# Moving the second horizontal product of a deformable convolution from VectorE to ScalarE, with the vertical mix one tap earlier

## What is computed

```
out_normal = conv(x, w_normal)
offset     = concat(conv(x, w_offx), conv(x, w_offy))       # 18 numbers a pixel
out_x      = deform_conv(x, offset, w_dx)
out_y      = deform_conv(x, offset, w_dy)
out        = relu(bn(conv(concat(out_normal, out_x, out_y), w_fusion)))
out        = relu(bn(conv(out, w_conv2)) + x)
# deform_conv: for each of 9 taps and each pixel, a bilinear sample
s = corner(y0, x0)*(1-ty)*(1-tx) + corner(y0, x0+1)*(1-ty)*tx
  + corner(y0+1, x0)*ty*(1-tx)   + corner(y0+1, x0+1)*ty*tx
out = einsum('bckhw,ock->bohw', s, w)
```

## Time and profile before

| what | value |
|---|---|
| median of 3 runs | 2600.68 us (2598.38 to 2600.81) |
| profiled execution, its own time | 2602.97 us |
| its span | 2601.2 us |
| busy in the span: PE, DVE, ACT, POOL | 91%, 87%, 60%, 74% |
| TensorE's granted clock, mean of the span | 0.961 |
| chain that ended last, by engine | DVE 46%, PE 23%, ACT 15%, issue 8%, DMA 5%, POOL 2% |

### The profile page before, as it was taken

One profiled execution on the slowest core, in us unless ns is written; L12 is line 12 of the kernel. 1 busy time (PEld: TensorE's weight loads), 2 busy tenths in 40 slices (PEclk: granted clock), 3 DMA queues, 4 the chain that ended last, 5 costly groups with the idle time before them and its releaser, 6 DMA issues.

```text
span 2601.2 us, 47091 instructions
## 1 busy us (share of the span) xinstructions
PE 2355.7 (91%) x15680; PEld 2319.4 (89%) x15680; DVE 2265.0 (87%) x5999; ACT 1561.9 (60%) x3577; POOL 1917.4 (74%) x1807
## 2 busy tenths in 40 slices
PE   3668999999999999999999999999999998999997
PEld 3668889898999999998999999999999998999997
DVE  5788988888999999999999989999999998999962
ACT  5777888778555555555555555555555555555531
POOL 7777777777777777777777777777777777777730
PEclk7789999999999999999999999999999999999998
DMA  7767777777777777777777777777777667776630
GB/s 232 220 208 219 235 228 231 232 231 229 227 237 233 231 234 237 233 236 232 236 237 237 234 237 239 238 222 210 209 209 217 206 208 212 210 210 210 202 111 26
DMA packets 179139, 564.90 MB, mean 217 GB/s; under 512 B 32720, under 2 KB 34128, under 8 KB 178768
## 3 DMA queue, kind: packets, MB, share of 16 engines
q0 software_dynamic: 144000, 471.97, 60.3%
q1 hardware_dynamic: 34896, 89.91, 10.1%
HBM read 527.41 MB, written 34.34 MB: 216 GB/s over the span
## 4 chain that ended last, share of the span: by engine, by line
DVE 46%; PE 23%; ACT 15%; issue 8%; DMA 5%; POOL 2%; ACTq 0%; DVEq 0%; SPq 0%; POOLq 0%
DVE mixed L756 11%; DVE d_lo L708 7%; DVE d_lo_f L832 7%; DVE samp L762 6%; ACT samp L535 6%; PE work L388 5%; PE work L394 5%; PE work L391 5%; DMA cells<-slope_table,index 4%; DVE samp_lo L708 4%; ACT samp_hi L534 3%; ACT mixed L535 3%; PE turned L431 2%; POOL cells L350 2%; PE acc L388 2%
## 5 line engine op out<-in xcount | busy, mean ns | idle before, releaser
L350 POOL DMA_INDIRECT cells<-slope_table,index x1350 | 1434.0, 1062 | 414.1 <-issue 223.3
L535 ACT ACTIVATE samp<-mixed,wgt 128x128 f32<-128x128 f32 x1800 | 644.6, 397 | 492.6 <-DVE mixed L756 490.8
L350 POOL DMA_INDIRECT cells<-in_xpair,index x450 | 473.7, 1053 | 166.6 <-issue 83.4
L756 DVE SCALAR_TENSOR_TENSOR mixed<-cells,wgt 128x256 f32<-128x256 f32 x1350 | 560.9, 477 | 39.2 <-DMA cells<-slope_table,index 37.9
L762 DVE SCALAR_TENSOR_TENSOR samp<-mixed,wgt,samp 128x128 f32<-128x128 f32 x1800 | 513.8, 345 | 39.1 <-ACT samp L535 38.8
L388 PE MATMUL work<-d_hi,w_hi 128*128 128x320 f32 x1440 | 467.9, 325 | 22.0 <-ACT off_s L534 19.7
L391 PE MATMUL work<-d_lo,w_hi 128*128 128x320 f32 x1440 | 452.8, 314 | 0.0
L394 PE MATMUL work<-d_hi,w_lo 128*128 128x320 f32 x1440 | 452.3, 314 | 0.0
L388 PE MATMUL acc<-samp_hi,w_hi 128*128 128x320 f32 x1440 | 450.2, 313 | 0.0
L391 PE MATMUL acc<-samp_lo,w_hi 128*128 128x320 f32 x1440 | 448.4, 311 | 0.0
L394 PE MATMUL acc<-samp_hi,w_lo 128*128 128x320 f32 x1440 | 446.9, 310 | 0.0
(11 more groups left out here) (86 smaller groups left out, 4279.3 us busy)
## 6 DMA issues: line engine op xcount, KB each, us to landing
cells<-slope_table,index POOLq DMA_INDIRECT x1350, 3.9
slope<-in_xpair SPq DMA_DIRECT2D x54, 384.0 KB, 5.3
slope_table<-slope SPq DMA_DIRECT2D x54, 384.0 KB, 4.1
x_raw<-in_xflat SPq DMA_DIRECT2D x40, 410.0 KB, 4.1
resid<-in_x SPq DMA_DIRECT2D x40, 320.0 KB, 5.3
out<-resid SPq DMA_DIRECT2D x40, 320.0 KB, 3.9
cells<-in_xpair,index POOLq DMA_INDIRECT x450, 3.8
w_lo_f<-in_weights SPq DMA_DIRECT2D x4, 576.0 KB, 7.9
```

The lines of the kernel that those rows point to most:

```text
L350: eng.indirect_dma_start(out=cells[:, g, :], out_offset=None, in_=cell_rows, in_offset=bass.IndirectOffsetOnAxis(ap=index[:, par, j, k:k + ...
L535: return eng.activation(dst, src, ACT.Copy, scale=scale)
L756: eng.scalar_tensor_tensor(out=both, in0=corner[:, g, :, 1, :], scalar=wgt[:, par, 1, 0, j, k:k + 1], in1=base, op0=ALU.mult, op1=ALU.add, ...
```

## The change

In images 1 to 3 (`n >= PLAIN`) ScalarE makes both horizontal products, in place in `mixed` (10 copies of 128 elements a tap), and VectorE adds them in a single instruction of 640 elements into `samp`. In image 0 the split stays as it was. `sample` is cut into `mix` and `blend`, and `mix` runs one tap earlier for all images: in step n VectorE does `blend(n + 2)`, `samples_low(n + 1)`, the indices if due, `mix(n + 3)`, and then its jobs. ScalarE does `samples_high(n + 1)`, then `across(n + 3)` and `upper(n + 4)`, and then its jobs. GpSimd, SyncE and TensorE keep their order; only the count that TensorE waits for differs (`samp_count`).

```diff
-                at_least(eng, samp_done, TILES * n + TILES)
+                at_least(eng, samp_done, samp_count(n + 1))
...
-            def left(n, k, par, tp):
-
-                at_least(eng, samp_turned, n - 1)
+            def across(n):
...
+                if n < PLAIN:
+                    at_least(eng, samp_turned, n - 1)
                 for j in range(TILES):
                     at_least(eng, mixed_done, TILES * n + j + 1)
-                    copy(samp[:, tp, j], mixed[:, tp, j, 0:C], scale=wgt[:, par, 0, 1, j, k:k + 1]).then_inc(left_done, 1)
+                    left, right = mixed[:, tp, j, 0:C], mixed[:, tp, j, C:2 * C]
+                    if n < PLAIN:
+                        copy(samp[:, tp, j], left, scale=wgt[:, c % 2, 0, 1, j, k:k + 1]).then_inc(left_done, 1)
+                    else:
+                        copy(left, left, scale=wgt[:, c % 2, 0, 1, j, k:k + 1]).then_inc(left_done, 1)
+                        copy(right, right, scale=wgt[:, c % 2, 1, 1, j, k:k + 1]).then_inc(left_done, 1)
...
                     n = i * TAPS + k
                     tp = (par + k) % 2
-                    if fl.strip and k < TAPS - 2:
-                        left(n + 2, k + 2, par, tp)
...
                     if fl.strip and (k < TAPS - 1 or fl.nxt):
                         samples_high(n + 1, 1 - tp)
...
-                        upper(n + 3, i, k + 3, par, 1 - tp)
...
+                    across(n + 3)
+                    upper(n + 4)
...
+            def blend(n):
...
+                if n >= PLAIN:
+                    at_least(eng, samp_turned, n - 1)
+                    at_least(eng, left_done, left_count(n + 1))
+                    combine(samp[:, tp], mixed[:, tp, :, 0:C], mixed[:, tp, :, C:2 * C], ALU.add).then_inc(samp_done, 1)
+                    return
...
-                        sample(n + 2, k + 2, par, tp)
...
+                    blend(n + 2)
                     if fl.strip and (k < TAPS - 1 or fl.nxt):
                         samples_low(n + 1, 1 - tp)
...
                     if k == fl.turn and fl.nxt:
                         indices(i + 1, 1 - par)
+                    mix(n + 3)
```

More of the change, by code:

```diff
@@ L63, with left_count, samp_count @@
 STEPS = NS + 4
+TOTAL = NS * TAPS
+PLAIN = STRIPS * TAPS
+def left_count(n):
+    return TILES * min(n, PLAIN) + 2 * TILES * max(n - PLAIN, 0)
+def samp_count(n):
+    return TILES * min(n, PLAIN) + max(n - PLAIN, 0)
 SLICES = [
@@ L557, in turned_evac, with upper @@
                     .then_inc(p_out, 1)
-            def upper(n, c, k, par, tp):
-                if c >= STRIPS:
+            def upper(n):
+                if n >= PLAIN:
                     return
-                at_least(eng, samp_done, TILES * (n - 1))
+                c, k, tp = n // TAPS, n % TAPS, n % 2
+                at_least(eng, samp_done, samp_count(n - 1))
                 for j in range(TILES):
@@ L567, in upper @@
                     copy(mixed[:, tp, j].rearrange("p (x c) -> p x c", x=2), corner[:, g, :, 0, :],
-                         scale=wgt[:, par, 0, 0, j, k:k + 1]).then_inc(upper_done, 1)
-            def left(n, k, par, tp):
-                at_least(eng, samp_turned, n - 1)
+                         scale=wgt[:, c % 2, 0, 0, j, k:k + 1]).then_inc(upper_done, 1)
+            def across(n):
+                if n >= TOTAL:
+                    return
+                c, k, tp = n // TAPS, n % TAPS, n % 2
+                if n < PLAIN:
+                    at_least(eng, samp_turned, n - 1)
                 for j in range(TILES):
                     at_least(eng, mixed_done, TILES * n + j + 1)
-                    copy(samp[:, tp, j], mixed[:, tp, j, 0:C], scale=wgt[:, par, 0, 1, j, k:k + 1]).then_inc(left_done, 1)
+                    left, right = mixed[:, tp, j, 0:C], mixed[:, tp, j, C:2 * C]
[4 more added lines that the diff above has]
+                        copy(right, right, scale=wgt[:, c % 2, 1, 1, j, k:k + 1]).then_inc(left_done, 1)
             def samples_high(n, tp):
@@ L597, in _ @@
             weights_high(W_DEF)
-            upper(0, 0, 0, 0, 0)
-            left(0, 0, 0, 0)
+            upper(0)
+            across(0)
             x_high(1, 1)
-            upper(1, 0, 1, 0, 1)
+            upper(1)
+            across(1)
+            upper(2)
             samples_high(0, 0)
-            left(1, 1, 0, 1)
-            upper(2, 0, 2, 0, 0)
+            across(2)
+            upper(3)
             eng.wait_ge(bn_step, 1)
@@ L625, in step @@
                     tp = (par + k) % 2
-                    if fl.strip and k < TAPS - 2:
-                        left(n + 2, k + 2, par, tp)
-                    elif fl.strip and fl.nxt:
-                        left(n + 2, k + 2 - TAPS, 1 - par, tp)
                     if fl.strip and (k < TAPS - 1 or fl.nxt):
@@ L633, in step @@
                         weights_high(fl.weights[k])
-                    if fl.strip and k < TAPS - 3:
-                        upper(n + 3, i, k + 3, par, 1 - tp)
-                    elif fl.strip and fl.nxt:
-                        upper(n + 3, i + 1, k + 3 - TAPS, 1 - par, 1 - tp)
                     if k == fl.turn and fl.nxt:
                         turned_evac(i + 1)
+                    across(n + 3)
+                    upper(n + 4)
                     if k == 1 and fl.last_row:
@@ L743, in indices, with combine, mix @@
                 eng.wait_ge(idx_ready, s + 1)
-            def sample(n, k, par, tp):
+            def combine(dst, a, b, op):
+                return eng.scalar_tensor_tensor(out=dst, in0=a, scalar=1.0, in1=b, op0=ALU.mult, op1=op)
+            def mix(n):
+                if n >= TOTAL:
+                    return
+                c, k, tp = n // TAPS, n % TAPS, n % 2
                 for j in range(TILES):
@@ L750, in sample @@
                     base = both
-                    if n < STRIPS * TAPS:
+                    if n < PLAIN:
                         at_least(eng, upper_done, TILES * n + j + 1)
                     else:
-                        at_least(eng, cells_in[g], (PER // GSLOTS * 16) * (n // TAPS) + 16 * turns)
+                        at_least(eng, cells_in[g], (PER // GSLOTS * 16) * c + 16 * turns)
                         base = corner[:, g, :, 0, :]
                     eng.scalar_tensor_tensor(
-                        out=both, in0=corner[:, g, :, 1, :], scalar=wgt[:, par, 1, 0, j, k:k + 1], in1=base,
+                        out=both, in0=corner[:, g, :, 1, :], scalar=wgt[:, c % 2, 1, 0, j, k:k + 1], in1=base,
                         op0=ALU.mult, op1=ALU.add,
                     ).then_inc(mixed_done, 1)
+            def blend(n):
+                if n >= TOTAL:
+                    return
+                c, k, tp = n // TAPS, n % TAPS, n % 2
+                if n >= PLAIN:
+                    at_least(eng, samp_turned, n - 1)
+                    at_least(eng, left_done, left_count(n + 1))
+                    combine(samp[:, tp], mixed[:, tp, :, 0:C], mixed[:, tp, :, C:2 * C], ALU.add).then_inc(samp_done, 1)
+                    return
                 for j in range(TILES):
@@ L763, in sample @@
                         out=samp[:, tp, j], in0=mixed[:, tp, j, C:2 * C],
-                        scalar=wgt[:, par, 1, 1, j, k:k + 1], in1=samp[:, tp, j], op0=ALU.mult, op1=ALU.add,
+                        scalar=wgt[:, c % 2, 1, 1, j, k:k + 1], in1=samp[:, tp, j], op0=ALU.mult, op1=ALU.add,
                     ).then_inc(samp_done, 1)
@@ L801, in _ @@
             weights_low(W_DEF)
-            sample(0, 0, 0, 0)
+            mix(0)
+            blend(0)
             x_low(1, 1)
-            sample(1, 1, 0, 1)
+            mix(1)
+            blend(1)
             samples_low(0, 0)
+            mix(2)
             eng.wait_ge(bn_in, 16)
@@ L828, in _ @@
             assert steps[0] == BN_STEPS
-            def combine(dst, a, b, op):
-                return eng.scalar_tensor_tensor(out=dst, in0=a, scalar=1.0, in1=b, op0=ALU.mult, op1=op)
             def sums(s):
@@ L905, in step @@
                         last_row(i - 2)
-                    if fl.strip and k < TAPS - 2:
-                        sample(n + 2, k + 2, par, tp)
-                    elif fl.strip and fl.nxt:
-                        sample(n + 2, k + 2 - TAPS, 1 - par, tp)
+                    blend(n + 2)
                     if fl.strip and (k < TAPS - 1 or fl.nxt):
```

## The result

The changed kernel takes 2811.05 us (median of 4 runs, 2810.56 to 2813.5), against 2600.74 for the kernel before: a ratio of 1.0815, 95% interval 1.0797 to 1.0832. The prediction was 2793, in a range from 2715 to 2900, and slower. The profiled execution took 2813.5 us, its span 2811.7.

A forecast was written before the change was run, and what follows sets the result against it. It took a per-step loop through VectorE and ScalarE to order the strip, with TensorE and VectorE near full and gathers at the strip's pace. 2603.0 + 114 + 75 = 2792, less 2.3, plus 3 for dips: 2793 us, range 2715 to 2900.

The forecast's parts named there:

- (c): New order in images 1 to 3: a loop through ScalarE and VectorE, 65.20 us a strip against 61.41, 114 us over 30 strips.
- load theory: Experiments' opposing view: ten ScalarE copies cause the loss, the order is harmless; new order with old split about 2600 us.
- Step 2: One of a strip's nine steps between `samp_lo` starts, ended by ScalarE with an offsets job of 1.21: 6.17 us.
- (e): TensorE: same work, 57.7 us fits the longer strips; two clock dips a strip expected, 1.7 us each, covered by slack.
- (a): VectorE's five horizontal instructions become one of 640 elements at 0.82 us: 0.58 us a tap less, 5.2 a strip.
- steps 5 and 7: The steps of a strip in images 1 to 3 that VectorE ends: priced 6.58 and 5.87 us.
- (b): ScalarE's five copies of 128 elements become ten: 2.94 us for ten, 13 us a strip more, fitting by busy time.
- Rival B: ScalarE's in-place copies don't overlap: 0.39 us each, 5.3 us a strip, 159 us, 2950 in all; chance 0.07.
- (d): Image 0 has the new order without VectorE's relief: 70.8 us a strip against 63.26, 75 us for ten strips.
- rival E: TensorE's clock: two or three uncovered dips a strip, 1.7 us each, 4.3 a strip over 40 strips, 2965; chance 0.05.
- Rival C: VectorE's relief wins: strips fall to TensorE's 57.7 us, 111 us less, 2490; chance 0.04.
- Rival D: No change: the gather stream, 45 × 1.369 = 61.6 us a strip, sets the time; 2601 with image 0 gather-bound; chance 0.04.

The follow-up runs named there:

- the order alone: New order with the old split of the horizontal products in all images, against the kernel before: 2724.3 us, ratio 1.0488.
- the split alone: New split (ten ScalarE copies, one VectorE sum) with the old order, against the kernel before: 2848.2 us, ratio 1.0965.
- the run with five sums: Changed kernel with the sum of the two products in five VectorE instructions of 128 elements instead of one of 640: 2836.9 us, 1.0909 to the kernel before.
- the hybrid: Image 0 in the old order, images 1 to 3 as the changed kernel with the mix ahead of the low part: 2610.6 us, 1.0033 to the kernel before.
- five sums of 128: The hybrid with five VectorE sums of 128 elements instead of one of 640: 2586.9 us, 0.9957 to the kernel before.

## Why the prediction was right, by its steps

**The loop, (c), held.** The run with the mix ahead of the low part shows it: ScalarE keeps its ten copies, VectorE's wait for `samp_hi` goes, and so does nearly all of the loss. With the order alone and the split alone, both slower, it leaves the load theory no place. Measured step by step, from one `samp_lo` start to the next in the strip from 1387.80 us on, against the prediction's: step 3 8.68 (8.74), step 4 8.84 (8.84), step 5 6.58 (6.58), step 6 9.30 (9.28), step 7 5.92 (5.87), step 8 7.29 (7.38), step 0 5.36 (5.42), step 1 7.01 (6.92). On average over the strips of images 1 to 3 step 6 takes 9.12, 0.16 under its price, and the others of this list stay within 0.1 of theirs. The sum came out 18 us short of the measured 2811, because both of its terms were short: 114 for 128 behind image 0, and 75 for 83 in it.

**Step 2 was priced 0.9 us too low**, at 6.17 where 7.08 was measured (1446.78 to 1453.86). The term counted ScalarE's offsets copy and then took `samp_hi` as ready. In the chain of waits of the changed kernel the path goes through TensorE instead (start us, length us, what):

```profile
1448.03 2.90 ACT mixed L549 x10
...
1450.97 0.41 ACT off_c L548
...
1451.39 0.43 ACT off_c L548
...
1451.83 0.43 ACT off_c L548
...
1452.32 0.78 PE turned L445 x5
...
1453.12 0.72 ACT samp_hi L548
...
1453.86 0.82 DVE samp_lo L727
```

TensorE waits for the offsets ahead of the transposes of the samples, and ScalarE's `samp_hi` needs those. Part (e) had said that TensorE has the room, which is so, but an order inside its list put a link into the loop. Moving that wait took 0.83 from step 2 and gave 0.66 us a strip.

**The relief of VectorE, (a)**, was sized rightly: 0.82 us for the 640-element sum, taken from the low part of that size, and 0.822 measured, 0.74 to the next instruction. In the changed kernel it counts almost only where VectorE ends a step, as the run with five sums shows: it takes back 0.27 a tap, and steps 5 and 7 grow by 0.29 and 0.27, the other seven by 0.14 together.

**The ten copies, (b)**, take 3.04 us from first to last end, 2.94 to the next instruction (1448.03 to 1450.97), as priced. Rival B, copies in place that don't overlap, is out by that row.

**Image 0, (d)**, came out at 72.25 a strip where I had 70.8, and 83 us in all where I had 75. The run with the order alone has the same image 0, so it is the order that costs there. The difference of 1.4 a strip can be placed by the starts of `samp_lo` in strips 6 to 8: step 2 takes 8.04 where 7.06 was priced, step 8 8.60 (8.27) and step 1 7.94 (7.81), and the other six agree with their prices to 0.01. So 1.0 of the 1.4 is step 2 again. With the wait for the offsets moved it takes 7.19, of which step 3 gives back 0.2. The 0.3 of step 8 and the 0.1 of step 1 stay open. For strips 0 to 3 the estimate was good: by the index for strip 4 the loss was 7.2 a strip.

**TensorE's clock, (e) and rival E.** Part (e) expected two dips a strip. At 1.7 us each, in strips of 65.84, they would give a mean granted clock of 0.95 (an estimate from the row that the prediction used). It was 0.99 from 1000 to 2400 us, against 0.98 before, so they hardly came; the steps there measure as priced without them. TensorE is idle 7.0 us a strip, as priced (1250.28 us busy of 1400), but it waits for `samp_lo` only 38 times in 27 strips, not in most steps; much of the rest stands behind ScalarE's `off_c`, `mid_f` and `raw`. In image 0 the granted clock was 0.94 from 350 to 700 us (0.99 before), and seven of the nine steps are explained without it; it may have a part in the other two.

**Rival C** (the relief wins) needed ScalarE's loop to open. The order that opens it brought the strips only from 61.41 to 61.05 and, in the hybrid, to 61.50, for the reason of rival D: the gather stream. The page on Perfetto Trace Analysis of the Trainium skill (section Optimizing Scalar/DVE Operations) says offloading to Scalar may make sense where DVE is saturated. VectorE was busy 277 of 300 us, and this case's runs don't bear the rule out as a forecast: the split alone made it 9.7% slower, and with the mix ahead of the low part images 1 to 3 stayed within 0.4 us a strip of before, since 45 gathers 1.36 to 1.37 us apart are as long as the strip.

**Rival D** is out in the changed kernel: from 800 to 2400 us the idle time ahead of a gather rose from 0.305 to 0.41 us (453.0 us ahead of 1,095). The gathers wait there; they set the pace only once the loop is shorter than 61.6 us.

## What to carry to other kernels

Before moving work from a full engine to a free one, write down the loop of one step through all engines and ask which engine ends it: what counts is what stands between the result of one engine and the start of the next, not the busy shares. An instruction moved earlier in the program should be put ahead of the one that waits for the partner engine, not behind it; here that one place was worth 180 us of 2,811. And look for a stream whose idle time ahead of each instruction stays at the same small amount whatever it is put down to (here 0.305 us ahead of each gather on average): it never pauses, so it may be the floor that a better order will meet.

## What the runs showed of the hardware

Gathers that take over 1.0 us fall together with VectorE's 640-element sum more often than the others: in the hybrid's timelines, from 800 to 2400 us, 38% of the long ones overlap such a sum by over 0.05 us and 8% of the short ones, while `samp_lo`, as long and with one input in PSUM, overlaps 14% and 36%. With five sums of 128 the shares for the sum are 37% and 27%. The Trainium skill, SBUF — State Buffer, section SBUF: two separate sides, tells of a port pair shared by VectorE and GpSimd, which a VectorE instruction with two SBUF inputs can hold for its whole length against a GpSimd instruction that reads SBUF. The shares agree with it. That the port is the cause wasn't tested by itself, nor that it costs time: the mean gather is 1.064 and 1.053 us in two runs with the single sum, and 1.048 with five.

Most of the gathers' excess over their median of 0.95 us stays open: it is not the bytes (half of them left the mean at 1.055), and not the room for descriptors (1.072 at half of it).
